# Query and key columns sorted by even and odd member, rotation without an exchange, rows scaled by ScalarE

## The reference, cut to what matters

```python
qkv = x @ w_qkv                      # 256 -> 768, 16 heads of 16 members
q, k, v = jnp.split(qkv, 3, axis=-1)
def _apply_rope(x, cos, sin):        # x: batch, head, token, member
    x_even = x[..., ::2]
    x_odd = x[..., 1::2]
    rot_even = x_even * cos - x_odd * sin
    rot_odd = x_odd * cos + x_even * sin
    return jnp.stack([rot_even, rot_odd], axis=-1).reshape(x.shape)
att = jnp.einsum('bhtd,bhsd->bhts', q, k) * scale
```

## Time and profile before

| | us |
|---|---|
| median of 3 runs | 1699.13 |
| lowest, highest | 1698.54, 1706.14 |
| the profiled execution, its own time | 1699.48 |
| its span | 1697.5 |
| VectorE, TensorE busy over the span | 1301.2, 1347.2 |
| ScalarE, GpSimd busy over the span | 1006.7, 383.1 |

### The profile page before, as it was taken

One profiled execution on the slowest core, in us unless ns is written; L12 is line 12 of the kernel. 1 busy time (PEld: TensorE's weight loads), 2 busy tenths in 40 slices (PEclk: granted clock), 3 DMA queues, 4 the chain that ended last, 5 costly groups with the idle time before them and its releaser, 6 DMA issues. The chain is left out here.

```text
span 1697.5 us, 28304 instructions
## 1 busy us (share of the span) xinstructions
PE 1347.2 (79%) x9622; PEld 601.7 (35%) x9622; DVE 1301.2 (77%) x1978; ACT 1006.7 (59%) x1339; POOL 383.1 (23%) x518
## 2 busy tenths in 40 slices
PE   5885698888888888888898986788827876579987
PEld 2443322222222222222222222566613333358754
DVE  6997677897778878888897952578667899485677
ACT  2554245686777867778786886456424656236642
POOL 3665010020110101111020110322100046600463
PEclk9897567998899989999999998999957888689999
DMA  6557501132130322303132022556744034576765
GB/s 194 186 190 237 112 4 24 21 73 41 28 83 5 73 40 36 74 8 75 36 73 40 9 43 77 173 166 204 220 136 131 25 118 156 180 248 207 247 202 197
DMA packets 159864, 186.28 MB, mean 110 GB/s; under 512 B 19572, under 2 KB 135796, under 8 KB 158708
## 3 DMA queue, kind: packets, MB, share of 16 engines
q1 hardware_dynamic: 153304, 167.65, 34.9%
q0 software_dynamic: 6144, 16.79, 3.0%
q10 hardware_dynamic: 288, 0.20, 0.1%
HBM read 100.94 MB, written 83.36 MB: 109 GB/s over the span
## 5 line engine op out<-in xcount | busy, mean ns | idle before, releaser
L1193 ACT ACTIVATE att_prob<-att_score,late_score_scale 128x1024 f32<-128x1024 f32 (+3 forms) x640 | 594.3, 987 | 222.3 <-PE att_score L1295 220.1
L1164 DVE TENSOR_REDUCE att_m_part<-att_mx 128x2 f32<-128x1024 f32 (+3 forms) x408 | 473.1, 1160 | 102.8 <-PE att_mx L1236 52.2
L1279 PE MATMUL att_pv<-att_prob,att_v 128*32 128x512 f32 (+3 forms) x2560 | 321.3, 576 | 0.5 <-POOL att_prob L1128 0.2
L1128 POOL TENSOR_SCALAR_AFFINE_SELECT att_prob<-att_prob 128x256 f32<-128x256 f32 x256 | 102.9, 407 | 770.6 <-ACT att_prob L1193 770.3
L1295 PE MATMUL att_score<-att_qop,att_kop 50*128 50x512 f16 (+3 forms) x1280 | 260.4, 368 | 8.9 <-ACT att_prob L1193 5.8
L1230 PE MATMUL att_mx<-att_kop,att_qop 48*128 48x512 f16 (+3 forms) x944 | 180.2, 366 | 104.9 <-DVE att_m_part L1164 99.8
L1164 DVE TENSOR_REDUCE att_m_part<-att_mx_one 128x1 f32<-128x384 f32 (+1 forms) x336 | 220.7, 657 | 36.2 <-PE att_mx_one L1230 28.8
L1295 PEld LDWEIGHTS att_score<-att_qop,att_kop 50*128 50x128 f16 x1280 | 69.7, 95 | 286.7 <-ACT att_prob L1193 189.4
L1230 PE MATMUL att_mx_one<-att_kop,att_qop 48*128 48x384 f16 (+1 forms) x336 | 134.3, 400 | 19.5 <-DVE att_m_part L1164 15.8
L2043 PE MATMUL rwkv_prod<-rwkv_xm,late_mixT 128*128 128x512 f32 x192 | 104.1, 699 | 33.3 <-ACT rwkv_kvr L2006 21.2
L1230 PEld LDWEIGHTS att_mx<-att_kop,att_qop 48*128 48x128 f16 x944 | 51.3, 96 | 174.8 <-DVE att_m_part L1164 157.5
(11 more groups left out here) (260 smaller groups left out, 2090.9 us busy)
## 6 DMA issues: line engine op xcount, KB each, us to landing
moe_xt<-rows SPq DMA_DIRECT2D x46, 256.0 KB, 3.3
results<-moe_y SPq DMA_DIRECT2D x46, 256.0 KB, 2.4
qk<-qkv_parts SPq DMA_DIRECT2D x32, 256.0 KB, 3.2
va<-qkv_v SPq DMA_DIRECT2D x8, 1024.0 KB, 5.5
att_v<-va SPq DMA_DIRECT2D x8, 1024.0 KB, 5.2
rows<-att_zeros SPq DMA_DIRECT2D x8, 864.0 KB, 6.2
att_kop<-qk SPq DMA_DIRECT2D x48, 128.0 KB, 4.9
att_qop<-qk SPq DMA_DIRECT2D x186, 32.0 KB, 3.0
```

The lines of the kernel that those rows point to most:

```text
L1128: nc.gpsimd.affine_select(out=at, in_=at, compare_op=ALU.is_ge, fill=0.0, base=0, pattern=[[0, 2], [1, P]], channel_multiplier=-1)\
L1164: nc.vector.tensor_reduce(cells[:, sides[0]:sides[-1] + 1, some], bank.rearrange("p a (h w) -> p a h w", w=w), AX.X, ALU.max).then_inc(m_f ...
L1193: nc.scalar.activation(prob[:, r % (PROBS * HP), :, n0:], score[:, r % 2, :, n0:], ACT.Exp, scale=late_weights.score_scale[:, 0:1])\
L1279: op = nc.tensor.matmul(pv[at, n0:], v[:, slot, j, at], prob[:, (st * HP + h // 2) % (PROBS * HP), h % 2, n0:], start=(j == 0), stop=(j == ...
```

## The change

The host sorts the 512 query and key columns of the weights: for queries and keys each, first the 128 even members of all heads, then the 128 odd ones. One block of 128 outputs then holds the even members and the next the odd members of the same pairs, at the same partitions. The scale 2^-12, which the copy `raw` applied, goes into the tables, and the tables lose the sign and hold a row for each pair. A group now has two units p (0 queries, 1 keys) of two blocks each; `QK` = 2 is their number.

- TensorE computes both blocks of a unit and makes no exchange; ScalarE copies both in one instruction of 128x1024 and makes no `swapped`.
- GpSimd multiplies each block by `cos` and by `sin`: four products of 128x512 a unit.
- VectorE makes `rot` of the even block by a subtraction and of the odd one by an addition, then one difference of 128x1024 a unit; the high half is one ScalarE copy of 128x1024.
- `LayerNorm` has a new mode, used here only: VectorE's chain ends with `shift` = -mean x `r` instead of the row scaling, and ScalarE scales the rows with `r` and `shift` (`scaled`).
- All queues get new orders; the rope tables are loaded, and the parts of the rows stored, one step later in SP's queue. The four stores of queries and keys write the rows of a block to eight members of each head.

```diff
+        if self.scalar:
+            dve.wait_ge(self.found, at + self.SMALL - 1)
+            nc.vector.scalar_tensor_tensor(self.shift[:, :], self.mv[:, :, 0], -1.0, self.r[:, :], ALU.mult, ALU.mult)\
+                .then_inc(self.found, 1)
+            return
...
+    def scaled(self, nc, act, n, slot, x):
+        act.wait_ge(self.found, (n + 1) * self.SMALL)
+        act.wait_ge(self.turn_done.sem, self.turn_done.freed(n, 2))
+        for j in range(TG):
+            op = nc.scalar.activation(self.xn[:, slot, j], x[:, j], ACT.Identity, bias=self.shift[:, j:j + 1],
+                                      scale=self.r[:, j:j + 1])
         op.then_inc(self.xn_done.sem, 1)
...
                 if at[0]:
                     load(*at[0])
                     if not at[1]:
                         load_weights()
-                    load_rope(*at[0])
+                if at[1]:
+                    load_rope(*at[1])
                 if at[1] and not at[2]:
                     late_weights.load(nc, sp, *late_ds)
-                if at[1]:
-                    store_xn(*at[1])
+                if at[2]:
+                    store_xn(*at[2])
...
+            def products(n, b, q):
+                pool.wait_ge(rope_in[b], q * 32 + 32)
+                for p in range(QK):
+                    c = n * QK + p
+                    pool.wait_ge(rot_done.sem, rot_done.freed(c, QK))
+                    pool.wait_ge(own_done.sem, own_done.done(c))
+                    for dst, table in ((by_cos, cos), (by_sin, sin)):
+                        for odd in range(KC):
+                            op = nc.gpsimd.tensor_tensor(dst[:, p, odd], raw[:, p, odd], table[:, b], ALU.mult)
+                    op.then_inc(turns_done.sem, 1)
...
             def step(at):
-                new, mid, old = at
...
+                ahead, new, mid = at
+                if ahead:
+                    scales(*ahead)
+                    if not new:
                         weights()
...
+                if new:
+                    low(*new)
+                if mid:
+                    rotated(*mid, 0)
+                    rotated(*mid, 1)
+                    last(*mid, 0)
+                    last(*mid, 1)
...
+                ahead, new, mid, old = at
+                if old:
+                    values(*old)
+                if new:
+                    high(*new)
                 if mid:
-                    values(*mid)
-
-            rolling(act, step, 3)
+                    own(*mid, 0)
+                if ahead:
+                    scaled(*ahead)
+                if mid:
+                    own(*mid, 1)
+                    first_part(*mid, 0)
+                    first_part(*mid, 1)
+
+            rolling(act, step, 4)
...
+                if new:
                     ln.turn(nc, pe, new[0], new[1], ident[:, :])
...
                 if mid:
                     pe.wait_ge(ln.lo_done.sem, ln.lo_done.done(mid[0]))
...
+                    heads(*mid, 0)
+                    heads(*mid, 1)
+                    values(*mid)
```

More of the change, by code:

```diff
@@ L206, with __init__ @@
     GUESS = 2.0 ** -((0x7FFFFFFF - 0x5F3759DF) / 2 ** 23)
[L208 removed]
+    def __init__(self, s, turned, full=False, scalar=False):
         self.turned = turned
+        self.scalar = scalar
+        if scalar:
+            self.SMALL = LayerNorm.SMALL + 1
+            self.shift = s.sb("ln_shift", [P, TG])
         self.stats = s.sb("ln_stats", [P, TG, 6])
@@ L658, in _ @@
             nc.gpsimd.memset(v[:, :, :, :, :, D:], 1.0).then_inc(set_done, 1)
[L660 to L672, removed]
+            def products(n, b, q):
+                pool.wait_ge(rope_in[b], q * 32 + 32)
+                for p in range(QK):
+                    c = n * QK + p
+                    pool.wait_ge(rot_done.sem, rot_done.freed(c, QK))
+                    pool.wait_ge(own_done.sem, own_done.done(c))
+                    for dst, table in ((by_cos, cos), (by_sin, sin)):
+                        for odd in range(KC):
+                            op = nc.gpsimd.tensor_tensor(dst[:, p, odd], raw[:, p, odd], table[:, b], ALU.mult)
+                    op.then_inc(turns_done.sem, 1)
+            in_groups(pool, products)
         @block.vector
         def _(dve):
-            ln.xn_done.open(dve)
             ln.lo_done.open(dve)
             rot_done.open(dve)
+            parts_done.open(dve)
             def weights():
                 dve.wait_ge(const_in, 16)
-                pairs = ident[:, :].rearrange("p (i two) -> p i two", two=2)
-                exchanged = exchange[:, :].rearrange("p (i two) -> p i two", two=2)
-                for one in range(2):
-                    op = nc.vector.tensor_copy(exchanged[:, :, one], pairs[:, :, 1 - one])
-                op.then_inc(exchange_set, 1)
                 w.vector(nc, dve, qk_ps[0:1, 0, 0, 0:P], qk_ps[:, 0, 0, P:P + 1], ident)
@@ L708, in normalise @@
[L708 to L711, removed]
-                        weights()
-                def low():
-                    n, b, q = new
-                    dve.wait_ge(v_done.sem, v_done.freed(n, 2))
-                    dve.wait_ge(xn_stored[b], q * 32 + 32)
-                    ln.low(nc, dve, n, b)
-                for stage, *m in ((rotated, 0), (statistics,), (rotated, 1), (normalise,), (last, 0), (rotated, 2),
-                                  (last, 1), (rotated, 3), (low,), (last, 2), (last, 3)):
-                    if not m and new:
-                        stage()
-                    if m and old:
-                        stage(old[0] * CH + m[0], m[0], old[1])
+                ahead, new, mid = at
@@ L829, in step @@
                     pe.wait_ge(ln.lo_done.sem, ln.lo_done.done(mid[0]))
-                first, second = range(0, TG // 2), range(TG // 2, TG)
-                for stage, *m in ((heads, 0), (heads, 1), (partners, 0), (heads, 2), (partners, 1), (turn,),
-                                  (partners, 2), (heads, 3), (values, first), (partners, 3), (values, second)):
-                    if not m and new:
-                        stage()
-                    if m and mid:
-                        stage(*mid, *m)
+                    heads(*mid, 0)
+                    heads(*mid, 1)
+                    values(*mid)
             rolling(pe, step, 2)
@@ L2601, in shape_tables @@
         1.0 / np.float32(10000.0) ** (np.arange(0, D, 2, dtype=np.float32) / np.float32(D))
-    ).astype(np.float32)[row % D // 2][:, None]
-    sign = np.where(row % 2 == 0, -1.0, 1.0)[:, None]
+    ).astype(np.float32)[row % (D // 2)][:, None]
     half = P // 2
```

148 lines of the change are left out of this document (68 added, 80 removed).

## The result

The changed kernel took a median of 1722.91 us (1721.7 to 1729.35, 4 runs) beside 1702.64 us for the kernel before (1698.54 to 1707.13, 4 runs): a ratio of 1.0126, interval 1.0084 to 1.0168, slower by more than 0.5%. The prediction was 1719.5 us, 1703 to 1730. Run again on another chip it took 1723.64 us (6 runs) against 1699.16, ratio 1.0138, interval 1.0106 to 1.0171. The profiled execution of after took 1729.35 us, its span is 1727.6.

What follows compares the result with a forecast made beforehand. VectorE, busy 136.1 of the first stage's 164 us, was taken to pace it. A later head and rounds of 19.65 against 17.4 us gave +20.0 on 1699.5: 1719.5 us, range 1703 to 1730.

Steps and rivals of the forecast that it cites:

- The stage alone, and the engines: First stage: its end moves the total one for one; removing TensorE's covered 37.3 us gains nothing; attention unchanged.
- Four small instructions blocked, one for each product: VectorE's chain each round: each of four GpSimd products lets one small instruction through; chain ends at 12.15 us.
- ScalarE's row scaling: ScalarE's queue each round: four scalings wait for `shift`, ahead of the second `raw` copy; 1.44 us, upper end 2.5.
- The head: Start of the stage: GpSimd's first product at 33.1 us instead of 26.55, behind group 1's scales and turn.
- The last stores: End of the stage, SP's queue: two stores at 0.6 us before `va`, issued at 178.9 against 158.88.
- the tail behind it is the same: End of the stage: time from the issue of the last `va` store onward unchanged, no cost.
- The sum: First stage: later head, five rounds of 19.65 us and two shorter groups give +20.0 us, total 1719.5.
- (A): Rival, VectorE's chain: small instructions run at 0.2 us under products, rounds 16.65 us, giving back 15: 1704.5 us; chance 0.15.
- (B): Rival, rounds: VectorE's load stays the pace, some 15.5 us a round, GpSimd's gaps 4 us shorter: 1691 us; chance 0.06.
- (C): Rival, rounds: sums of p = 0 fall under products, 1724.5 us, or 1730 with slow row scalings; chance 0.17.
- The rule on the ports: Ports shared by GpSimd and VectorE: a waiting VectorE instruction gets its turn between two products, ahead of queued products.
- the order in which none passes: VectorE's chain: queued products count as earlier, chain ends at 12.95 us, sum 4 us longer; chance 0.1.

Runs made afterwards that it cites:

- experiment 5: Changed kernel with each query and key matmul on TensorE done twice, same result: 1722.63 us (one run); the stage ends 2.8 us later.
- experiment 3: Changed kernel plus a wait: GpSimd's products of a group start only after VectorE's chain for two groups ahead: 1771.12 us, ratio 1.0128 on a slower chip.
- experiment 1: Changed kernel with ScalarE's `raw` copy for p = 1 moved ahead of the row scalings: 1763.65 us, ratio 1.0082 on a slower chip.
- experiment 2: Changed kernel with ScalarE's `raw` copy for p = 0 moved ahead of the values and the high half: 1763.72 us, ratio 1.0084 on a slower chip.
- experiment 4: Changed kernel with the row scalings put back on VectorE, behind its chain: 1773.76 us, ratio 1.0153 on a slower chip.
- version 6: Changed kernel with VectorE making the cosine products, GpSimd only the sine products, and new queue orders: 1691.35 us, ratio 0.9947; again 1682.98 us, ratio 0.9885.
- version 7: version 6 with the wait for ScalarE's row scaling moved to just before `r` is written: 1677.16 us, ratio 0.9864 to the kernel before.

## Why the prediction was right

**The stage alone, and the engines.** Right. 26.2 us in the stage, and -1.7 behind attention. That TensorE's freed 37.3 us are worth nothing is borne out by experiment 5. Attention was 5.6 us longer in the first profile of after and 1.3 in the second, each against the kernel before's. Over all profiles of kernels whose attention code is the same it lies between 931.6 and 951.4, so differences of this size say nothing of the change.

**Four small instructions blocked, one for each product.** Right, by the timeline of after, in five rounds out of five, and by experiment 3. A gap of 5.77 (5.65 predicted), the end of the chain 77.69 - 65.59 = 12.10 us after the last product (12.15 predicted).

**ScalarE's row scaling.** The one term of the round that was mis-sized. I took 1.44 us for four, from the value copies; measured is 79.71 - 77.72 = 1.99. For the same 128x256 that is 0.50 us each against 0.36. Two things differ: the values have their input in PSUM and the rows theirs in SBUF, and the rows take a bias beside the scale. Which of them costs the time was not tried; two casts of 128x1024 in the timeline of after differ by 0.06 us only, 0.95 from SBUF (66.96 to 67.91) and 0.89 from PSUM (69.35 to 70.24), so the memory is hardly all of it. It lies within the bounds, 1.44 to 2.5, and I took the end that had the same shape. It costs 0.55 in each of five rounds; the other terms give 0.1 back: 20.11 against 19.65, +2.4 us.

**The head.** First product at 34.73, 33.1 predicted. ScalarE's and TensorE's rows:

```profile
11.25 2.07 ACT L282 ACTIVATE qkv_ln_xn<-qkv_xin,qkv_ln_shift,qkv_ln_r 128x256 f32<-128x256 f32 x4
```

```profile
27.81 1.94 PE L292 MATMUL qkv_turned<-qkv_ident,qkv_ln_xn 128*128 128x128 f32 x8 [10.64 <-ACT qkv_ln_xn L282]
```

The same term enters twice, once for each group's rows, and with the waits around it the turn stands at 27.81 instead of 26.2. From the turn to the first product the prediction had 6.9 us and the trace 6.92. The head is +1.6 us. The change itself makes it 8.2 us longer than before, close to a third of the loss, and experiments 1 to 3 leave that as it is. The row of the turn names it: TensorE waits 10.64 us for the rows of group 1, and the heads of group 0 stand behind that turn. With the scaling back on VectorE (experiment 4) the first product starts at 33.29; in versions 6 and 7, where TensorE multiplies a group in the step in which it turns it, at 29.57 and 30.68; that order was not tried alone.

**The last stores.** Twice not counted. The prediction had two stores to issue before `va`; all four were still to come, and took 2.57 us of SP's queue where 1.2 were counted, and from the last product to the issue of `va` it took 0.5 us more than predicted. SyncE's queue:

```profile
180.87 2.57 SPq L632 DMA_DIRECT2D qk<-qkv_parts  x4
183.48 0.65 SPq L635 DMA_DIRECT2D va<-qkv_v  x1
```

And "the tail behind it is the same" was wrong: from the issue of `va` to the next stage it took 190.25 - 183.48 = 6.8 us against 5.1. The transfers view puts the landing of `va` at 6.3 us after its issue, 4.6 before. Before, the issue of the four stores ahead of it was spread over 5.85 us; here the four, 1 MB in all, are issued in 2.57 us just ahead of `va`. That this is why it lands later was not tried alone; version 7, with the same stores, has 6.7.

**The sum.** 20.0 predicted; 1.6 (head) + 2.4 (rounds) + 0.5 (issue) + 1.6 (landing) more gives 26.1, against 26.2 in the stage. The median moved by 20.3 us, in the second comparison by 24.5, so the forecast 1719.5 is nearer to 1722.91 than its terms were to the trace. That is luck: the stage moved by 6 us more than forecast, and the second comparison is nearer to the stage than to the forecast. Nearly all of the 6 us went one way: what I had not priced was a cost.

**The rivals.** (A), the chain escaping the products: no, in no round of after. Its mechanism is real where it is arranged. Its price, 16.65 us a round, was about right: the round of experiment 1 ahead of which the chain ran nearly free took 16.5. Experiment 3 gave 5.2 us of the 15, and it buys the free chain with a wait: the first gap is 8.23 us there against 5.65. (B), VectorE remaining the bound and faster: the two gaps that it needed 4 us shorter together were 5.77 and 4.48 instead of 5.65 and 4.2. What it says about the load of VectorE is what versions 6 and 7 then used. (C): the sums of p = 0 ended at 80.13, 0.64 ahead of the products; they had more room than the 0.15 us predicted, because the longer row scaling held the products back. The row scaling came out halfway to its upper end.

**The rule on the ports.** Each of the four queued products of a burst let one VectorE instruction through, in the round shown, and eight let eight through in experiments 1 and 4, at 1.11 to 1.19 us each. So the order in which none passes, to which the prediction gave 0.1, is out. The Trainium skill, SBUF — State Buffer, section Who interferes with whom, says that who issues first has the pair of ports; the trace agrees, if a waiting instruction counts as issued and a product still in the queue does not.

## What to carry to other kernels

Removing work from an engine that isn't the bound bought nothing here, and moving it cost: write out one round of every queue, with each wait, before counting busy time. A chain of small dependent VectorE instructions must not lie under GpSimd's long ones; put statistics and instructions that read PSUM there, and if need be make GpSimd wait. When an order is changed, look again at every wait that was free because somebody else was late (the one buffer of `r` was worth 1.6 us a round).

## What the runs showed that I had not expected

- A wait that was added made the stage 5.2 us shorter (experiment 3).
- ScalarE needs 0.50 us for 128x256 float32 values from SBUF with a scale and bias for each row, and 0.36 for the same size from PSUM with a scale (1.99 / 4 and 1.44 / 4); whether the memory or the bias makes the difference was not separated.
- Under a running product of 128x512 these VectorE instructions kept their time: `ln_lo` at 1.21 to 1.23 us, the cosine products of 128x1024 from PSUM at 1.17, statistics at 1.40 for four. An instruction of 128x4 with all data in SBUF took 1.11 to 1.24 instead of 0.16, a sum of 128x512 1.74 instead of 0.68.
- TensorE's granted clock in the stage fell from 0.91 to 0.84 without the exchange and was 0.89 with the matmuls doubled; between the last two a round did not change.
- The executions of one kernel (version 6) lay up to 23 us apart, 1670.18 and 1693.33, as much as the whole gain of version 7.
